# A fused Mamba, MLP and mixture layer on one core: weight splits moved in their block, narrow products with both weight halves side by side, last down products by tile

## The chip, the cores and the metric

The kernel runs on one NeuronCore of one Trainium2 chip. The metric is the device time of one execution in microseconds, as the median of several runs. Times inside an execution come from one profiled execution and are counted from the start of its span.

## The reference

The input is x, 8 sequences of 256 tokens with 512 channels, in float32.

```python
x = x + layernorm(attn(layernorm(x)))     # Mamba-2 block, then a gated MLP, each with a residual
x = x + layernorm(ffn(layernorm(x)))      # linear layer plus one of 4 rank-8 adapters for each token

# inside attn
zxbcdt = rmsnorm(h) @ w_in.T              # z, xs, B, C and dt (4 heads: 4 columns)
conv over 4 taps, silu; dt = softplus(dt + dt_bias)
chunks of 128 tokens: y = (C B' * decay) (x dt) + C state exp(cs) + D x
h = h + (y * silu(z)) @ w_out.T
h = h + (silu(h2 @ gate.T) * (h2 @ up.T)) @ down.T      # 1792 inner channels

# inside ffn
logits = x @ gate_w.T + bias; one_hot = argmax          # 4 columns
z = x @ lora_A.T                                        # 32 columns, masked by one_hot
out = x @ W_up.T + z_masked @ lora_B
```

The result must have about float32 precision. So every large product is made of float16 halves: each float32 operand is held as a high and a low float16 part, and a product is the sum of high x high, high x low and low x high.

## The kernel before

**Groups and steps.** A group is one sequence: 256 tokens, two tiles of 128. Three groups are in work at once, each in another branch. `steps` runs t from 1 to 9 with a = t (Mamba branch), b = t - 1 (MLP branch) and c = t - 2 (adapter branch); a branch whose group does not exist is left out. Step 1 has a = 1 and b = 0 and no c; step 8 has b = 7 and c = 6 and no a. Before step 1 the function `first` does the Mamba branch of group 0, and after step 8 the function `last` does what is left of groups 6 and 7.

**Blocks.** Each step has 14 blocks f, one for each 128 of the 1792 MLP channels. The order of work is written out by hand, once for each engine: a block has the MLP work of b first, then what the tables `A_AT`, `C_AT` and `NEXT_AT` name for this f. Nothing but this order and the semaphores schedules the work.

- TensorE, block f: `b_gu(b, f)`, 24 matmuls of 256 columns for gate and up (tiles gu0 and gu1, in turn); `b_down(b, f - 2)`, 6 matmuls of 512 columns, 3 for each token tile j, into acc0 and acc1; then the tables. After block 13 come the down products 12 and 13 together.
- ScalarE: `b_silu` (L782, sg from gu), `b_hi` (L792, high half of act), then the tables.
- VectorE: `b_prod` (L1220, sg times the up part), `b_lo` (L1225, low half of act), then the tables.

For one f this is a chain: TensorE's gate/up, silu on ScalarE, product on VectorE, high half on ScalarE, low half on VectorE, down product on TensorE. The gate/up product of block f waits for `b_prod` of block f - 2, since there are two gu banks.

**Weight splits.** The weights are scaled and split into halves on the chip: `upper_halves` (L630) on ScalarE and `lower_halves` (L1004) on VectorE, 56 units of 128x512. Part of them is made in `first`. The rest is made in step 1 by `prepare(f)`, called in each block f when a == 1: blocks 0 to 9 split gate and up of block f + 4 and down of block f + 1 (3 units), block 10 three down units, block 11 the four of the linear layer and the small gl_w, blocks 12 and 13 two units each of w_out (L643 and L1016), and block 13 the adapter matrices lora_b (`prep_lora`, VectorE, L990 to L996). A low half waits for its high half; in blocks 12 and 13 a high half also waits for the low half before it. Before the change `prepare(f)` stands between the MLP work of the block and the tables.

**The Mamba branch in a step.** TensorE makes the xs, B, C and z products (`a_in`, `a_z`, tile wa) in blocks 0 to 3, and in block 1 `a_dt`, the product for dt: for each token tile and each of the 4 k blocks three matmuls of 4 columns into tile wc. VectorE turns it into dts (`a_dtv`, L1096), ScalarE does abs, exp and ln (L707 to L709) in block 2, VectorE the rest of softplus (L1105 to L1116) and a_t. TensorE needs a_t for the two running sums in block 3 (`a_cs`, tri and a_t). These go over HBM and back, and ScalarE makes the decays in block 5 (L735, L725). VectorE multiplies them by dt (L1126) and by the attention products (`a_att`, L1135; the second in block 6). TensorE makes `a_state`, `a_y(0)` and `a_y(1)` in block 7; `a_y(1)` needs the second attention product. In block 7 VectorE forms y and, from group 2 on, its largest value, and from it y_diag (L1156, tile tok). TensorE spreads this over the partitions in block 8 (`a_y_spread`, ones x tok), so that y can be scaled and split in halves for the output projection (`a_o`, block 10). `a_hi1` and `a_lo1` (L662 and L1071, block 11) split the rows of the next group, which the DMA transposes into ht; TensorE needs ht in block 13 (`a_in(g + 1, 0)`). `a_hi2` and `a_lo2` (L767, L1208, block 12) do the same for h2t, which the next step's `b_gu` reads. `a_conv(g + 1, 0)` on ScalarE (L679, block 13) writes the buffer from which h2t was transposed, and waits for that transfer.

**The adapter branch.** `c_logits` (block 6) makes logits and z in one product with 36 columns, three matmuls for each tile and k. `c_route` (VectorE, block 6, L1308 to L1339) adds the bias, finds the first largest logit, masks z by `hot` and splits it into three bfloat16 parts, which TensorE transposes in block 7 (`c_zt`, L1720).

**The end.** In `last` VectorE waits for acc0 (semaphore `acc0_ready`), computes `b_mlp(7, 0)` (L1237), statistics and norms for tile 0 and then for tile 1, and the adapter branch of group 7 follows tile by tile.

The product functions before:

```python
PAIRS = [(0, 0), (0, 1), (1, 0)]
todo = [(lf[a], rt[b]) for lf, rt in zip(lefts, rights) for a, b in PAIRS]
for n, (lf, rt) in enumerate(todo):
    last = mm(dst, lf, rt, start and n == 0, stop and n == len(todo) - 1)
```

## Time and profile before

| | us |
|---|---|
| median of 3 runs (lowest, highest) | 768.98 (768.39, 773.36) |
| the profiled execution | 769.4 |
| its span | 767.7 |
| mean granted clock of TensorE in it | 0.986 of 2.4 GHz |
| TensorE busy | 733.9 |
| VectorE busy | 500.0 |
| ScalarE busy | 343.8 |

The span is the time between the first and last instruction; the profiled execution's own time is 1.7 us longer. A busy TensorE means that a matmul was in the array; a granted clock of 1.00 is 2.4 GHz and 0.50 is 1.2 GHz. All matmuls that go through the helper `mm` carry one line, L1478, so they are told apart by tile and shape. PE is TensorE, PEld its weight loads, DVE VectorE, ACT ScalarE, POOL GpSimd.

### The profile page before, as it was taken

To read this page: it belongs to the slowest core of one execution; us is meant where nothing else is said; L and a number is where in the kernel's file an instruction comes from. 1 tells how busy PE (TensorE), PEld (TensorE's weight loads), DVE (VectorE), ACT (ScalarE), POOL (GpSimd) and SP (SyncE) were. 2 spreads that over 40 slices of the span, in tenths; PEclk is the share of its full clock that TensorE was granted. 3 is DMA by queue.
4 is the path that set the end of the run, shared out by engine and by line. 5 is a ranking of instruction groups with operands and counts; after the bars stand their busy time and mean duration, and the time that the engine had idled before them with its cause. 6 is when DMAs were issued, how large, how long until landed. Compare 5 with 4: busy or idle time off the path is not lost.

```text
span 767.7 us, 14108 instructions
## 1 busy us (share of the span) xinstructions
PE 733.9 (96%) x5620; PEld 527.1 (69%) x5620; DVE 500.0 (65%) x1181; ACT 343.8 (45%) x671; POOL 133.1 (17%) x187
## 2 busy tenths in 40 slices
PE   4999898989999999999999999999999999999995
PEld 3867676667766877578666876578766876677752
DVE  5898868787655758367665757467674767365356
ACT  2854775446533373335633374245633265323211
POOL 2220211004110311105110311104210131001021
PEclk9999989999999999999999999999999999999997
DMA  8970010030204030040303120040303211032001
GB/s 310 386 255 1 2 55 1 1 83 29 56 1 83 28 83 3 0 111 3 81 1 56 56 58 27 1 110 2 83 1 41 71 35 22 1 83 49 9 1 55
DMA packets 61202, 44.82 MB, mean 58 GB/s; under 512 B 45848, under 2 KB 46032, under 8 KB 61136
## 3 DMA queue, kind: packets, MB, share of 16 engines
q1 hardware_dynamic: 61136, 43.92, 20.3%
q8 instruction: 44, 0.72, 0.4%
q14 instruction: 22, 0.18, 0.1%
HBM read 28.68 MB, written 4.22 MB: 43 GB/s over the span
## 4 chain that ended last, share of the span: by engine, by line
PE 70%; DVE 13%; ACT 8%; issue 4%; DMA 2%; SPq 1%; POOL 0%; ACTq 0%; DVEq 0%
PE gu L1478 30%; PE wa L1478 19%; PE acc L1478 15%; PE wc L1478 6%; ACT dec L735 2%; DVE xbc L1082 2%; DVE sg L1220 1%; DMA weights<-in_w_gate 1%; ACT L782 1%; DVE weights L1004 1%; DVE y L1143 1%; DMA ht<-ra 1%; ACT weights L630 1%; ACT sg L782 1%; DVE y_scales L1154 1%
## 5 line engine op out<-in xcount | busy, mean ns | idle before, releaser
L1478 PE MATMUL gu<-h2t,weights 128*128 128x256 f16 x2688 | 314.5, 274 | 1.0 <-DVE h2t L1214 1.0
L1478 PEld LDWEIGHTS gu<-h2t,weights 128*128 128x128 f16 x2688 | 263.4, 99 | 46.9 <-issue 5.1
L1478 PE MATMUL acc<-weights,act 128*128 128x512 f16 x672 | 161.7, 379 | 0.0
L1220 DVE SCALAR_TENSOR_TENSOR sg<-gu,bound,sg 128x256 f32<-128x256 f32 x112 | 53.3, 476 | 94.6 <-ACT sg L782 94.5
L782 ACT ACTIVATE sg<-gu,scale_inv 128x256 f32<-128x256 f32 x112 | 52.8, 471 | 134.5 <-PE gu L1478 134.3
L1478 PE MATMUL wa<-ht,weights 128*128 128x256 f16 x912 | 107.1, 275 | 4.0 <-DMA ht<-ra 3.7
L1478 PEld LDWEIGHTS acc<-weights,act 128*128 128x128 f16 x672 | 65.6, 98 | 57.7 <-DVE act L1225 0.3
L1478 PEld LDWEIGHTS wa<-ht,weights 128*128 128x128 f16 x912 | 89.7, 99 | 20.6 <-DMA ht<-ra 4.7
L792 ACT ACTIVATE act<-sg 128x256 f16<-128x256 f32 x112 | 46.6, 416 | 103.5 <-DVE sg L1220 103.5
L1225 DVE TENSOR_TENSOR act<-sg,act 128x256 f16<-128x256 f32 x112 | 49.7, 444 | 54.0 <-ACT act L792 54.0
L1082 DVE SCALAR_TENSOR_TENSOR xbc<-wa,conv_ws,xbc 128x253 f32<-128x253 f32 (+1 forms) x132 | 57.4, 476 | 1.6
L1004 DVE SCALAR_TENSOR_TENSOR weights<-weights,scale_v 128x512 f16<-128x512 f32 x56 | 39.9, 765 | 3.0 <-ACT weights L630 2.8
L491 POOL TENSOR_SCALAR small_c<-mv_c 128x2 f32<-128x2 f32 x21 | 4.0, 191 | 205.5 <-DVE mv_c L1026 205.5
L630 ACT ACTIVATE weights<-weights,scale_v 128x512 f16<-128x512 f32 x56 | 36.1, 708 | 0.7 <-DVE scale_v L953 0.7
L679 ACT ACTIVATE xbc<-wa,cols_t,conv_ws 128x256 f32<-128x256 f32 x48 | 24.3, 557 | 26.4 <-PE wa L1478 22.5
L520 POOL TENSOR_SCALAR y<-xbc,rows_t 128x256 f32<-128x256 f32 x28 | 30.7, 1109 | 26.0 <-ACT xbc L690 26.0
L1478 PE MATMUL wc<-weights,h3t 128*128 128x512 f16 x144 | 33.0, 379 | 0.0
L1478 PE MATMUL wa<-w_out_t,ra 128*128 128x512 f16 x144 | 32.1, 379 | 0.0
L491 POOL TENSOR_SCALAR small_a<-mv_a 128x2 f32<-128x2 f32 (+1 forms) x22 | 5.2, 235 | 150.9 <-DVE mv_a L1026 97.5
L760 ACT ACTIVATE hn<-h 128x512 f32<-128x512 f32 x16 | 10.1, 631 | 37.9 <-DVE h L1186 26.1
L512 POOL TENSOR_TENSOR hn<-tri,dts 128x512 f32<-128x512 f32 x16 | 17.9, 1140 | 48.2 <-DVE a_t L1116 48.2
L1478 PE MATMUL acc<-weights 128*128 128x128 bf16 x224 | 15.8, 228 | 10.4 <-DMA weights<-in_w_in 7.9
(242 smaller groups left out, 830.1 us busy)
## 6 DMA issues: line engine op xcount, KB each, us to landing
xa<-in_x SPq DMA_DIRECT2D x9, 512.0 KB, 3.7
ra<-cs_rows SPq DMA_DIRECT2D x7, 512.0 KB, 3.5
weights<-in_x SPq DMA_DIRECT2D x7, 512.0 KB, 3.8
out_x<-h SPq DMA_DIRECT2D x14, 256.0 KB, 2.1
weights<-in_w_in SPq DMA_DIRECT2D x5, 512.0 KB, 6.7
weights<-in_w_down SPq DMA_DIRECT2D x3, 768.0 KB, 12.9
weights<-in_w_gate SPq DMA_DIRECT2D x2, 1024.0 KB, 13.1
weights<-in_w_up SPq DMA_DIRECT2D x2, 1024.0 KB, 13.7
```

The lines of the kernel that those rows point to most:

```text
L512: nc.gpsimd.tensor_tensor(tdt[:, j], tri[:].unsqueeze(1).broadcast_to([P, H, P]), dts[:, 4, j].unsqueeze(2).broadcast_to([P, H, P]), ALU.m ...
L520: nc.gpsimd.tensor_scalar(y[:, h], xbc[:, 0], rowt[:, 4 + h:5 + h], None, ALU.mult)\
L630: nc.scalar.activation(Wh[:, u, 0], W[:, u + SHIFT], ACT.Copy, scale=sv[:, t:t + 1])\
L679: nc.scalar.activation(xbc[:, c], src[:, m * SEQ:(m + 1) * SEQ], ACT.Identity, bias=conv_b[:, c:c + 1], scale=cw[:, c * TAPS + TAPS - 1:c ...
L735: nc.scalar.activation(dec[:, j, h], ra[:, j, h], ACT.Relu, bias=cs_col[:, j, h:h + 1], scale=-1.0) .then_inc(sem("fall_ready"), 1)
L782: nc.scalar.activation(sg[:, f % 2], GU[f % 2][:, 0:SEQ], ACT.Silu, scale=inv_gate)\
L792: nc.scalar.activation(act[:, slot(f), 0], sg[:, f % 2], ACT.Copy)\
L1004: nc.vector.scalar_tensor_tensor(Wh[:, u, 1], W[:, u + SHIFT], sv[:, t:t + 1], Wh[:, u, 0], ALU.mult, ALU.subtract).then_inc(split, 1)
L1082: ins = nc.vector.scalar_tensor_tensor(xbc[:, c, late:], conv_in(g, c)[:, 0:SEQ - late], cw[:, c * TAPS + k:c * TAPS + k + 1], xbc[:, c, l ...
L1220: nc.vector.scalar_tensor_tensor(sg[:, f % 2], GU[f % 2][:, SEQ:2 * SEQ], up_to_act, sg[:, f % 2], ALU.mult, ALU.mult).then_inc(sem("prod_ ...
L1225: nc.vector.tensor_tensor(act[:, slot(f), 1], sg[:, f % 2], act[:, slot(f), 0], ALU.subtract)\
L1478: return nc.tensor.matmul(dst, left, right, start=start, stop=stop)
```

## The change

There are three edits.

1. `prepare(f)` on ScalarE and VectorE is called at the end of the block, behind the three tables, in step 1 (a == 1).
2. `a_dt` and `c_logits` use `narrow_product`. For each tile and k there are two matmuls in place of three: the high half of the tokens times both halves of the weights, which lie side by side (8 or 72 columns), and the low half of the tokens times the high half (4 or 36 columns) into the first part. The sum of the two parts is left to VectorE: a second operation in `a_dtv`, and in `c_route` a copy and an addition of 72 columns for each tile; the logits are then read from SBUF. The masking by `hot` is done in two operations, one for each tile.
3. For the last group the four down products left at the end are ordered by tile: (12, 0), (13, 0), (12, 1), (13, 1) in place of (12, 0), (12, 1), (13, 0), (13, 1).

```diff
@@ scalar and vector, step @@
-                    if a == 1:
-                        prepare(f)
                     if a is not None and f in A_AT:
                         A_AT[f](a)
                     if c is not None and f in C_AT:
                         C_AT[f](c)
                     if a is not None and a + 1 < GROUPS and f in NEXT_AT:
                         NEXT_AT[f](a + 1)
+                    if a == 1:
+                        prepare(f)
...
@@ vector, a_dtv @@
-                nc.vector.scalar_tensor_tensor(
-                    dts[:, 0], WC[:, 0:TILES * H].rearrange("p (t h) -> p t h", h=H), inv_dt,
-                    rowt[:, 8:12].unsqueeze(1).broadcast_to([P, TILES, H]), ALU.mult, ALU.add)\
+                src = WC[:, 0:2 * TILES * H].rearrange("p (t s h) -> p t s h", t=TILES, s=2)
+                chain_a(nc.vector.scalar_tensor_tensor(
+                    dts[:, 0], src[:, :, 1], inv_dt, rowt[:, 8:12].unsqueeze(1).broadcast_to([P, TILES, H]),
+                    ALU.mult, ALU.add))
+                nc.vector.scalar_tensor_tensor(dts[:, 0], src[:, :, 0], inv_dt, dts[:, 0], ALU.mult, ALU.add)\
                     .then_inc(sem("dtv_ready"), 1)
...
@@ vector, c_route @@
-                src = WC[:, 0:TILES * (E + E * R)].rearrange("p (t n) -> p t n", t=TILES)
+                n = E + E * R
+                src = WC[:, 0:2 * TILES * n].rearrange("p (t s n) -> p t s n", t=TILES, s=2)
+                chain_c(nc.vector.tensor_copy(z_low[:], src[:, :, 1]))
+                nc.vector.tensor_tensor(zs[:], src[:, :, 0], z_low[:], ALU.add).then_inc(sem("zs_ready"), 1)
+                dve.wait_ge(sem("zs_ready"), g + 1)
                 chain_c(nc.vector.scalar_tensor_tensor(
-                    lg[:], src[:, :, 0:E], inv_gl, rowt[:, 12:16].unsqueeze(1).broadcast_to([P, TILES, E]),
+                    lg[:], zs[:, :, 0:E], inv_gl, rowt[:, 12:16].unsqueeze(1).broadcast_to([P, TILES, E]),
                     ALU.mult, ALU.add))
-                nc.vector.tensor_copy(zs[:], src[:, :, E:]).then_inc(sem("zs_ready"), 1)
...
-                zv = zs[:].rearrange("p t (e r) -> p (t e) r", r=R)
-                hv = hot[:].rearrange("p t e -> p (t e)").unsqueeze(2).broadcast_to([P, TILES * E, R])
-                chain_c(nc.vector.tensor_tensor(zv, zv, hv, ALU.mult))
+                for t in range(TILES):
+                    zv = zs[:, t, E:].rearrange("p (e r) -> p e r", r=R)
+                    ins = nc.vector.tensor_tensor(zv, zv, hot[:, t].unsqueeze(2).broadcast_to([P, E, R]), ALU.mult)
+                    chain_c(ins, wait=t == TILES - 1)
...
@@ tensor @@
+            def narrow_product(dst, n, lefts, rights):
+
+                for k, (lf, rt) in enumerate(zip(lefts, rights)):
+                    mm(dst, lf[0], rt, k == 0, False)
+                    last = mm(dst[:, 0:n], lf[1], rt[:, 0], False, k == len(lefts) - 1)
+                return last
...
-            def b_down(g, f):
+            def b_down(g, f, js=range(TILES)):
...
-                for j in range(TILES):
+                for j in js:
...
-                last.then_inc(sem("down_done"), 1)
+                    if j == TILES - 1:
+                        last.then_inc(sem("down_done"), 1)
...
-                if b is not None:
+                if b is not None and alone(b):
+
+                    for f, j in ((FBLK - 2, 0), (FBLK - 1, 0), (FBLK - 2, 1), (FBLK - 1, 1)):
+                        b_down(b, f, [j])
+                elif b is not None:
                     for f in range(FBLK - BEHIND, FBLK):
                         b_down(b, f)
```

**Order on VectorE, step 1, block 2.** Before: the splits of weights, then the convolution of xbc, then softplus on dts and a_t.

```order
L1004 SCALAR_TENSOR_TENSOR weights<-weights,scale_v 128x512 x3
L1082 SCALAR_TENSOR_TENSOR xbc<-wa,conv_ws,xbc 128x253 x2
L1082 SCALAR_TENSOR_TENSOR xbc<-wa,conv_ws,xbc 128x254 x2
L1082 SCALAR_TENSOR_TENSOR xbc<-wa,conv_ws,xbc 128x255 x2
L1105 TENSOR_SCALAR dts<-dts 128x8
L1110 TENSOR_TENSOR dts<-dts 128x8
L1108 SCALAR_TENSOR_TENSOR dts<-dts 128x8 x3
L1111 TENSOR_TENSOR dts<-dts 128x8
L1112 SCALAR_TENSOR_TENSOR dts<-dts 128x8
L1113 TENSOR_TENSOR dts<-dts 128x8
L1115 SCALAR_TENSOR_TENSOR dts<-dts 128x8
L1116 TENSOR_TENSOR a_t<-dts,neg_a 128x8
```

Now the same stretch of VectorE (the lines have moved by 1 to 3):

```order
L1083 SCALAR_TENSOR_TENSOR xbc<-wa,conv_ws,xbc 128x253 x2
L1083 SCALAR_TENSOR_TENSOR xbc<-wa,conv_ws,xbc 128x254 x2
L1083 SCALAR_TENSOR_TENSOR xbc<-wa,conv_ws,xbc 128x255 x2
L1108 TENSOR_SCALAR dts<-dts 128x8
L1113 TENSOR_TENSOR dts<-dts 128x8
L1111 SCALAR_TENSOR_TENSOR dts<-dts 128x8 x3
L1114 TENSOR_TENSOR dts<-dts 128x8
L1115 SCALAR_TENSOR_TENSOR dts<-dts 128x8
L1116 TENSOR_TENSOR dts<-dts 128x8
L1118 SCALAR_TENSOR_TENSOR dts<-dts 128x8
L1119 TENSOR_TENSOR a_t<-dts,neg_a 128x8
L1005 SCALAR_TENSOR_TENSOR weights<-weights,scale_v 128x512 x3
```

The three splits have moved from ahead of the convolution to behind a_t. The same holds for every block of step 1.

**Order on ScalarE, step 1, from block 12 on.** Before (w_out_t are the high halves of w_out, xbc<-hn the rows for h2t, xbc<-wa the first taps of group 2):

```order
L643 ACTIVATE w_out_t<-w_out_t,scale_v 128x512 x2
L767 ACTIVATE xbc<-hn,sumsq 128x512 x2
L782 ACTIVATE sg<-gu,scale_inv 128x256
L792 ACTIVATE act<-sg 128x256
L643 ACTIVATE w_out_t<-w_out_t,scale_v 128x512 x2
L679 ACTIVATE xbc<-wa,cols_t,conv_ws 128x256 x2
```

Now:

```order
L768 ACTIVATE xbc<-hn,sumsq 128x512 x2
L644 ACTIVATE w_out_t<-w_out_t,scale_v 128x512 x2
L783 ACTIVATE sg<-gu,scale_inv 128x256
L793 ACTIVATE act<-sg 128x256
L680 ACTIVATE xbc<-wa,cols_t,conv_ws 128x256 x2
L644 ACTIVATE w_out_t<-w_out_t,scale_v 128x512 x2
```

In block 12 the rows for h2t come first, and in block 13 the taps, which wait for h2t's transfer, now stand ahead of the last two halves of w_out.

**Order on TensorE, the last down products of group 7**, with the semaphores that they wait for. Before:

```order
L1478 MATMUL acc<-weights,act 128x512 [waits act_ready]
L1478 MATMUL acc<-weights,act 128x512 x5
L1478 MATMUL acc<-weights,act 128x512 [waits act_ready]
L1478 MATMUL acc<-weights,act 128x512 x5
L1478 MATMUL wa<-weights,h3t 128x512 [waits zt_ready]
```

Now:

```order
L1484 MATMUL acc<-weights,act 128x512 [waits act_ready]
L1484 MATMUL acc<-weights,act 128x512 x2
L1484 MATMUL acc<-weights,act 128x512 [waits act_ready]
L1484 MATMUL acc<-weights,act 128x512 x2
L1484 MATMUL acc<-weights,act 128x512 [waits act_ready]
L1484 MATMUL acc<-weights,act 128x512 x2
L1484 MATMUL acc<-weights,act 128x512 [waits act_ready]
L1484 MATMUL acc<-weights,act 128x512 x2
L1484 MATMUL wa<-weights,h3t 128x512 [waits zt_ready]
```

Two runs of six have become four of three: the first two end tile 0, the others tile 1.

## Rows read from the trace of the kernel before

**Rows 1.** The page: busy time of each engine, share of the span, instructions.

```profile
PE 733.9 (96%) x5620; PEld 527.1 (69%) x5620; DVE 500.0 (65%) x1181; ACT 343.8 (45%) x671; POOL 133.1 (17%) x187
```

**Rows 2.** Waits of TensorE's matmuls: us in total, times, longest.

```profile
PE wa L1478 <- DMA ht<-ra: 3.7, 2, 3.1
PE wc L1478 <- DVE a_t L1116: 3.3, 1, 3.3
...
PE wa L1478 <- DVE dec L1135: 2.2, 1, 2.2
```

**Rows 3.** Waits of TensorE's weight loads, same columns.

```profile
PEld wa L1478 <- DVE tok L1156: 3.5, 6, 0.6
```

**Rows 4.** Waits of VectorE between 73 and 167 us, same columns.

```profile
DVE sg L1220 <- ACT sg L782: 6.8, 6, 2.5
DVE act L1225 <- ACT act L792: 6.8, 14, 0.5
DVE dec L1126 <- ACT dec L725: 2.5, 1, 2.5
```

**Rows 5.** TensorE in time: start, length (us), instruction, idle before.

```profile
94.74 0.60 PE L1478 MATMUL wc<-tri,a_t 128*8 128x128 f32 x2 [3.30 <-DVE a_t L1116]
...
95.71 5.11 PE L1478 MATMUL gu<-h2t,weights 128*128 128x256 f16 x24
...
119.83 1.13 PE L1478 MATMUL wa<-dec,tok 128*128 128x512 f32 x2 [2.21 <-DVE dec L1135]
...
186.42 0.39 PE L1478 MATMUL wc<-tri,a_t 128*8 128x128 f32 x2
```

**Rows 6.** VectorE in time, steps 1 and 2.

```profile
92.71 0.17 DVE L1105 TENSOR_SCALAR dts<-dts 128x8 f32<-128x8 f32 x1 [0.78 <-ACT dts L709]
...
117.10 2.08 DVE L1004 SCALAR_TENSOR_TENSOR weights<-weights,scale_v 128x512 f16<-128x512 f32 x3 [0.19 <-ACT weights L630]
...
166.86 0.48 DVE L1220 SCALAR_TENSOR_TENSOR sg<-gu,bound,sg 128x256 f32<-128x256 f32 x1
...
185.67 0.17 DVE L1116 TENSOR_TENSOR a_t<-dts,neg_a 128x8 f32<-128x8 f32 x1
```

**Rows 7.** ScalarE in time, step 1.

```profile
86.51 1.93 ACT L630 ACTIVATE weights<-weights,scale_v 128x512 f16<-128x512 f32 x3
...
162.12 1.02 ACT L679 ACTIVATE xbc<-wa,cols_t,conv_ws 128x256 f32<-128x256 f32 x2 [0.98 <-DMA h2t<-xbc]
```

**Rows 8.** Windows of 1 us: busy TensorE, granted clock, DMA share, GB/s.

```profile
122.00:123.00 1.00, 1.00 (x7) 0.50 0.00 0
...
154.00:155.00 1.00, 0.00 (x0) 1.00 1.05 191
```

**Rows 9.** TensorE in time, step 3.

```profile
260.07 0.74 PE L1478 MATMUL wc<-dt_w,ht 128*128 128x4 f16 x24
260.68 2.78 PE L1478 MATMUL gu<-h2t,weights 128*128 128x256 f16 x24
...
288.18 0.76 PE L1478 MATMUL wc<-gl_w,h3t 128*128 128x36 f16 x24
...
300.67 0.49 PE L1478 MATMUL wa<-tok,ones 128*128 128x128 f32 x2
```

**Rows 10.** VectorE in time, step 3, route and the next product.

```profile
291.94 0.22 DVE L1308 SCALAR_TENSOR_TENSOR logits<-wc,scale_inv,rows_t 128x8 f32<-128x8 f32 x1
...
292.34 0.15 DVE L1312 TENSOR_REDUCE mx<-logits 128x2 f32<-128x8 f32 x1
...
293.79 0.23 DVE L1330 TENSOR_TENSOR zs<-zs,hot 128x64 f32<-128x64 f32 x1
...
295.00 0.48 DVE L1220 SCALAR_TENSOR_TENSOR sg<-gu,bound,sg 128x256 f32<-128x256 f32 x1
```

**Rows 11.** The chain that ended last: start, us, what.

```profile
736.80 3.25 PE acc L1478 x15
```

**Rows 12.** VectorE in time, the end.

```profile
740.17 0.75 DVE L1237 SCALAR_TENSOR_TENSOR weights<-acc,bound,h1b 128x512 f32<-128x512 f32 x1 [1.44 <-PE acc L1478]
```

More of the change, by code:

```diff
@@ L209, in build @@
         lg = sb("logits", [P, TILES, E])
-        zs = sb("zs", [P, TILES, E * R])
-        zr = sb("zr", [P, TILES, E * R])
+        zs = sb("zs", [P, TILES, E + E * R])
+        z_low = sb("z_low", [P, TILES, E + E * R])
+        zr = z_low[:, :, E:]
         zp = sb("z_parts", [P, TILES, 8, E * R], BF16)
@@ L1335, in c_route @@
                 prev(g, 1, 1, dve, sem("zt_ps_ready"))
[L1336 to L1339 removed]
+                chain_c(nc.vector.tensor_copy(zp[:, :, 2:5], copies(zs[:, :, E:], 3)))
+                chain_c(nc.vector.tensor_tensor(zr, zs[:, :, E:], zp[:, :, 2], ALU.subtract))
+                chain_c(nc.vector.tensor_copy(zp[:, :, 0:2], copies(zr, 2)))
+                nc.vector.tensor_tensor(zp[:, :, 5], zr, zp[:, :, 0], ALU.subtract)\
                     .then_inc(sem("zm_ready"), 1)
@@ L1380, in step @@
                         NEXT_AT[f](a + 1)
+                    if a == 1:
+                        prepare(f)
                 if a is not None:
@@ L1560, in a_dt @@
                 for j in range(TILES):
-                    last = split_product(WC[:, j * H:(j + 1) * H], [tokens(ht, k, j) for k in range(KB)],
-                                         [[dt_w[:, s, k] for s in range(2)] for k in range(KB)])
+                    last = narrow_product(WC[:, 2 * j * H:2 * (j + 1) * H], H, [tokens(ht, k, j) for k in range(KB)],
+                                          [dt_w[:, :, k] for k in range(KB)])
                 last.then_inc(sem("dt_ps_ready"), 1)
@@ L1709, in c_logits @@
                         pe.wait_ge(sem("last_t3_split"), j + 1)
-                    last = split_product(WC[:, j * n:(j + 1) * n], [tokens(h3t, k, j) for k in range(KB)],
-                                         [[gl_w[:, s, k] for s in range(2)] for k in range(KB)])
+                    last = narrow_product(WC[:, 2 * j * n:2 * (j + 1) * n], n, [tokens(h3t, k, j) for k in range(KB)],
+                                          [gl_w[:, :, k] for k in range(KB)])
                 last.then_inc(sem("lg_ps_ready"), 1)
```

11 lines of the change are left out of this document (2 added, 9 removed).

## The prediction

> **What bounds the kernel now.** I read the page first: TensorE is busy 96% of the span [rows 1], so a microsecond counts only where TensorE waits, works at half its clock, or does less. Then the waits of TensorE: apart from loads at the start and the tail there are three long ones, on a_t, on dec and on the transposed ht [rows 2]; all three lie in step 1, the step in which the weights are still being split. The waits of the weight loads show one more, small and regular: 3.5 us in 6 pieces on tok, written at L1156 [rows 3]. That is y_spread (L1478, ones x y_diag), once in each of steps 2 to 7. So in these steps VectorE's chain up to y_diag ends just after TensorE gets there. Everywhere else in steps 2 to 8 TensorE sets the pace.
>
> The times below are of the profiled execution: 767.7 us of span, 769.4 us in all, 0.4 above the median of 768.98. I work out differences and take them off the median.
>
> **The weight splits at the end of each block (step 1).** Nothing is added: each block of 3 splits (2.08 us on VectorE [rows 6], 1.93 us on ScalarE [rows 7]) is done later within its block. TensorE needs a gate or up slot four blocks and a down slot three blocks after its split, so a move within the block does not make it wait. What moves up is the other branch's work.
>
> First wait, 3.30 us on a_t [rows 2, 5]. The chain to a_t in block 2 passes one block of splits on each engine. ScalarE's softplus steps start 1.84 us earlier, and VectorE's first step after them (92.71, after 0.78 us of waiting for ScalarE [rows 6]) comes at about 90.95. TensorE starts at 93.0 instead of 94.74. That is 1.76 us, and with 0.2 us less of its own work before, its wait is still 1.8 us.
>
> Second wait, 2.21 us on dec [rows 5]. The second attention product on VectorE stands behind the splits of block 6, which start at 117.10 and take 2 us [rows 6]. Before it, ScalarE's exponentials in block 5 no longer stand behind splits, and going block by block ScalarE and VectorE gain 1.9 us up to there. The product ends about 115.6 and y(1) starts near 115.7, 4.1 us earlier. But TensorE, pulled forward too and at full clock, would be there at 113.1: its wait is 2.6 us, not gone.
>
> Third wait, 3.1 us on ht [rows 2]. The low halves of the next group's rows stand behind four splits in block 11, and after the move behind none. In my walk VectorE is 3 to 5 us ahead by then, ht lands about 148.1, and TensorE waits 0.3 us for it, so it starts step 2 earlier by much more than VectorE does: its first gate/up product could start 6.5 us earlier.
>
> What is late next: VectorE. Its work in step 1 is the same, it can only give up idle time: 6.8 us before sg and 2.5 us before dec, while the 6.8 us in 14 pieces before act are a round trip to ScalarE that stays [rows 4]. Two things take some of it back. In block 10 the splits used to fill the wait for the output projection, and now follow it. In block 13 ScalarE now does the next group's first taps before the last w_out halves; these taps wait for the landing of h2t (0.98 us even before [rows 7]), and VectorE's low halves and all of the lora preparation queue behind them. From both I get VectorE's first product of step 2 (166.86 [rows 6]) 2.9 us earlier, not 6.5. VectorE then works nearly without a break to a_t of step 2 (185.67 [rows 6]), which TensorE meets at 186.42 [rows 5] with some 0.5 us to spare. With the extra operation of a_dtv (0.25 us) a_t comes 2.65 us earlier; TensorE, 6.7 us earlier, waits 3.4 us and goes on at 183.2. The term is **-3.2 us**. Ends: 0, if each gain only turns into a wait, and -6.7, if TensorE keeps all of it.
>
> The clock. Behind the first wait 24 gate/up matmuls took 5.11 us instead of 2.78 [rows 5, 9], and behind the second the granted clock read 0.50 (1.2 GHz); behind the third, the second longest, it stayed at 1.00 (2.4 GHz) [rows 8]. So a wait of this length may or may not cost clock. (The Trainium skill, "TensorE: Matmul & The Clock Gate", section "What's actually happening", says that the same kernel slows differently from run to run, by the phase at its start; the trace agrees in that like waits had unlike outcomes.) My walk has three candidates: 2.6 us before y(1), about 2.4 us before the last down product of step 1 (the low half in block 13), and 3.4 us on a_t of step 2. A spell at half clock costs between nothing, where a wait follows, and the 2.3 us by which the gate/up block grew. I take **+1.7 us** for one that counts; ends 0 and +5.
>
> **Products with both halves side by side.** For dt, 24 matmuls of 4 columns take 0.61 us from their start to that of the next block [rows 9], 25 ns each. Now 16 of 4 or 8 columns: 8 x 25 = 0.20 us less. The logits' 24 matmuls of 36 columns take 0.76 us with the end of the last [rows 9], about the same spacing. Of the new 16, 8 have 72 columns; 256 columns take 109 ns (24 in 2.78 us with the end of the last [rows 9], 2.62 without), so 72 take between 25 and 109 ns, by proportion 31. That saves 0.15 us; at 109 ns it would cost 0.47.
>
> (The Trainium skill, same page, section "Back-to-back issue gap", says that in a stream of weight loads and matmuls the loads count too, about 81 ns a pair at 128 columns. By that the 128 pairs saved would be worth 10.4 us; the trace has whole pairs at 25 ns.)
>
> The price is on VectorE. a_dtv has a second operation, about 0.25 us, hidden before z(0) in steps 3 to 7 (ScalarE waits for TensorE there). In c_route the logits and the copy take 0.40 us before (291.94 to 292.34 [rows 10]). Now there are a copy of 72 columns and an addition, each like an operation on these tiles with its wait, 0.26 us, and the logits from SBUF, 0.20: 0.72 in all, +0.32. The masking by hot, 0.26 us in one operation before, is two of half the width, the first without a wait: +0.07. Together **+0.39 us** per step; ends 0.1 (the operations overlap) and 0.8 (each new one costs a full 0.26). VectorE's next product follows without a gap (295.00 [rows 10]), then y, y_top and y_diag, for which TensorE already waits [rows 3], and which it starts at 300.67 [rows 9]. So in steps 2 to 7 all of it lands on the path: 6 x 0.39 = **+2.3 us**, and the 0.15 us of the logits only lengthens TensorE's wait there, 0.58 to about 1.1 us by the weight loads. Saved on the path: dt in steps 3 to 7, 5 x 0.20 = **-1.0 us**; the logits of step 8, which has no y_spread, and of the tail, **-0.25 us**. At the start the dt product's gain and the second a_dtv operation cancel.
>
> **Last down products tile by tile.** acc0 was ready after 15 matmuls, which take 3.25 us, 0.217 each [rows 11], and VectorE, idle 1.44 us, waited for it at 740.17 [rows 12]. Now it is ready after 12: 0.65 us earlier, if the last block's act is there: VectorE ended its low half 1.44 us before 740.17, at 738.73 [rows 12], and TensorE comes to it 9 matmuls after 736.80, at 738.75. VectorE then works without a gap for several microseconds, and the later waits of TensorE shorten with it: **-0.65 us**. Ends: 0 and -0.7. In the tail c_route's extra 0.39 us is hidden behind 18 matmuls of the linear product.
>
> **Sum.** -3.2 + 1.7 + 2.3 - 1.0 - 0.25 - 0.65 = -1.1 us: 768.3 for the profiled execution, 767.9 for the median.
>
> **The rivals.** (a) VectorE keeps up: its waits in step 1 vanish, a_t of step 2 is not late, TensorE keeps 6.7 us and no clock is lost. For it: 9.3 us of idle time that can go [rows 4]. Against it: VectorE's unbroken work from the low halves to a_t, and the taps waiting for h2t. -6.7 + 2.3 - 1.25 - 0.65 = -6.3: 762.7 us. (b) Slower: the waits collect in one place, a_t of step 2, where TensorE stands 3.4 us and the clock falls behind it as it did at 94.74, after another fall at y(1). It decides once the clock costs 2.8 us more than nothing; with 5 us it gives +2.2, 771.2 us. For it: two of the three waits of step 1 cost clock. Against it: a fall inside step 1 is partly taken up by the next wait. (c) c_route's operations overlap, or y_spread has slack that the trace hides: without the +2.3, 765.6 us. Against it: six like waits. (d) Whole pairs cost what the page says: up to 10.4 us less, 759 us; the rows speak against it.
>
> **How the numbers follow.** Forecast 0.60, (a) 0.11, (b) 0.16, (c) 0.11, (d) 0.02. The forecast's own range is 766.2 (no clock lost) to 770. To hold 8 in 10 with parts of (a), (b) and (c) on both sides I take 764.5 to 771. One per cent, 7.7 us, is about what a measurement of this kernel can tell from no change. Below 761.3 us only (d) and a generous (a) lead: 0.04. Above 776.7 would take a wait that I have not found: 0.03. Within 1%: 0.93.
>
> **What would show it.** In the changed profile: the wait on a_t in step 1 near 1.8 us and a new one on a_t near 3.4 us in step 2; the wait before y(1) still there; ht no longer waited for; the weight loads' waits on tok, six pieces, near 1.1 us each; the time from one y_spread to the next in steps 3 to 7 longer by 0.2 us; the last group's first DVE result 0.65 us closer to the last gate/up block. I am wrong if step 2 starts a_t without a wait (then (a)), if the tok waits stay at 0.6 us (then (c)), or if the clock stays below 1.00 for over 6 us behind new waits (then (b)).

## The result, and the profile after

The changed kernel took 774.39 us in the median of 8 runs (772.72 to 775.99), beside 771.75 us for the kernel before (8 runs, 768.39 to 773.36): ratio 1.0042, 95% interval 1.0025 to 1.0060. That is slower by 1.9 to 4.6 us; the prediction had 1.1 us faster. The three runs of before shown ahead of the prediction lay 2.8 us below that median. All comparisons below are ratios to runs of before on the same chip at the same time; 0.001 is 0.77 us.

The page of the kernel after, its first lines, beside [rows 1]: VectorE is busy 5.7 us longer and GpSimd 3.4 us, though GpSimd's program is the same.

```profile
span 774.0 us, 13868 instructions
...
PE 735.8 (95%) x5492; PEld 525.9 (68%) x5492; DVE 505.7 (65%) x1205; ACT 343.2 (44%) x671; POOL 136.5 (18%) x187
```

The waits of TensorE after (matmuls, then weight loads; total, times, longest), beside [rows 2, 3]. The wait on ht in step 1 is all but gone (0.2 us); a_t in step 1 is shorter, dec (before y(1)) longer; act, a second a_t and the matmuls' waits on tok are new.

```profile
PE wa L1484 <- DVE tok L1159: 4.3, 6, 0.7
...
PE wc L1484 <- DVE a_t L1119: 3.4, 2, 2.2
...
PE wa L1484 <- DVE dec L1138: 2.7, 1, 2.7
PE acc L1484 <- DVE act L1228: 2.2, 1, 2.2
...
PEld wa L1484 <- DVE tok L1159: 7.3, 6, 1.2
```

TensorE in time after, steps 1 and 2, beside [rows 5].

```profile
72.72 5.41 PE L1484 MATMUL gu<-h2t,weights 128*128 128x256 f16 x48 [0.98 <-DVE h2t L1217]
96.44 0.39 PE L1484 MATMUL wc<-tri,a_t 128*8 128x128 f32 x2 [2.21 <-DVE a_t L1119]
121.27 2.08 PE L1484 MATMUL wa<-dec,tok 128*128 128x512 f32 x2 [2.74 <-DVE dec L1138]
155.42 2.79 PE L1484 MATMUL wa<-ht,weights 128*128 128x256 f16 x24 [0.21 <-DMA ht<-ra]
161.67 2.39 PE L1484 MATMUL acc<-weights,act 128*128 128x512 f16 x6 [2.16 <-DVE act L1228]
189.96 0.39 PE L1484 MATMUL wc<-tri,a_t 128*8 128x128 f32 x2 [1.20 <-DVE a_t L1119]
```

Step 1 starts at 72.72; before it started at 69.73, with this row:

```profile
69.73 3.45 PE L1478 MATMUL gu<-h2t,weights 128*128 128x256 f16 x30 [0.98 <-DVE h2t L1214]
```

Over the profiled runs of this study, whose code up to there differs at most in dt, this start lies anywhere from 69.73 to 74.17. So times in step 1 are counted from it. From it to the product on a_t of step 2 it is 117.24 us, before 186.42 - 69.73 = 116.69: the wait on ht went and nothing was gained. From one y_spread to the next, called a period below, it is 87.70 us (305.00 to 392.70) against 87.42 before; two of the five periods after were longer, 88.76 and 88.12, each with a wait on ht (0.90 and 0.24 us), and one of before, 88.20. And the granted clock, beside [rows 8], is down in a third place, behind the new wait on act (windows of 1 us, same columns):

```profile
122.00:123.00 1.00, 1.00 (x2) 0.50 0.06 16
154.00:155.00 1.00, 1.00 (x6) 1.00 0.87 162
163.00:164.00 1.00, 1.00 (x4) 0.50 0.59 227
```

By windows of 2 us the clock was low for 3.4 us in each of the three places, before for 6.8 behind a_t and 3.4 behind dec: 10.2 us either way.

VectorE in time after, step 3, beside [rows 10]: from the end of the attention product to its next gate product 3.54 us (295.78 to 299.32), before 3.06 (291.94 to 295.00).

```profile
295.78 0.23 DVE L1312 COPY z_low<-wc 128x72 f32<-128x72 f32 x1
296.04 0.23 DVE L1313 TENSOR_TENSOR zs<-wc,z_low 128x72 f32<-128x72 f32 x1
296.31 0.23 DVE L1315 SCALAR_TENSOR_TENSOR logits<-zs,scale_inv,rows_t 128x8 f32<-128x8 f32 x1
296.57 0.16 DVE L1318 TENSOR_REDUCE mx<-logits 128x2 f32<-128x8 f32 x1
...
298.04 0.29 DVE L1335 TENSOR_TENSOR zs<-zs,hot 128x32 f32<-128x32 f32 x2
...
299.32 0.48 DVE L1223 SCALAR_TENSOR_TENSOR sg<-gu,bound,sg 128x256 f32<-128x256 f32 x1
```

VectorE's waits after between 73 and 167 us, beside [rows 4]. Of the 6.8 us on sg 0.2 are left, but now VectorE waits longer for ScalarE's splits and for the output projection. All its waits in that stretch, the smaller ones too, add up to 22.5 us before and 22.0 after.

```profile
DVE act L1228 <- ACT act L793: 6.8, 14, 0.5
DVE w_out_t L1017 <- ACT w_out_t L644: 3.6, 3, 2.1
DVE weights L1005 <- ACT weights L631: 3.5, 3, 1.5
DVE dec L1129 <- ACT dec L726: 2.9, 1, 2.9
DVE h L1191 <- PE wa L1484: 2.7, 1, 2.7
```

And its splits took longer. VectorE's splits of gate, up, down and the linear layer as a group (busy us, mean ns of one), of the kernel before, then of the kernel after:

```profile
L1004 DVE SCALAR_TENSOR_TENSOR weights<-weights,scale_v 128x512 f16<-128x512 f32 x56 | 39.9, 765 | 3.0 <-ACT weights L630 2.8
```

```profile
L1005 DVE SCALAR_TENSOR_TENSOR weights<-weights,scale_v 128x512 f16<-128x512 f32 x56 | 42.3, 806 | 4.5 <-ACT weights L631 4.4
```

The chain at the end, beside [rows 12], first the last gate/up block of before, then the rows after: VectorE starts on acc0 5.74 us after the start of the last gate/up block (740.13), before 6.16 (740.17 - 734.01). But the clock in the tail then was down for 6.8 us, before for 3.4, and the whole tail came out no shorter.

```profile
734.01 2.78 PE L1478 MATMUL gu<-h2t,weights 128*128 128x256 f16 x24
```

```profile
740.13 2.78 PE L1484 MATMUL gu<-h2t,weights 128*128 128x256 f16 x24
...
745.87 0.75 DVE L1240 SCALAR_TENSOR_TENSOR weights<-acc,bound,h1b 128x512 f32<-128x512 f32 x1 [1.01 <-PE acc L1484]
```

### The profile page after: what moved, and what is told of

Same layout as the page of the kernel before. It is cut to its first block, busy times and chain, and to the rows that moved or that the text cites. A ratio compares the mean times of both kernels' runs of the same rounds, so it can differ in the third digit from the quotient of the medians.

```text
span 774.0 us, 13868 instructions
## 1 busy us (share of the span) xinstructions
PE 735.8 (95%) x5492; PEld 525.9 (68%) x5492; DVE 505.7 (65%) x1205; ACT 343.2 (44%) x671; POOL 136.5 (18%) x187
## 4 chain that ended last, share of the span: by engine, by line
PE 63%; DVE 19%; ACT 8%; issue 5%; DMA 2%; SPq 1%; POOL 0%; ACTq 0%; DVEq 0%
PE gu L1484 26%; PE wa L1484 17%; PE acc L1484 14%; PE wc L1484 6%; DVE weights L1005 3%; DVE xbc L1083 3%; ACT dec L736 2%; DVE sg L1223 2%; DVE y L1146 1%; ACT act L793 1%; DMA ht<-ra 1%; DMA weights<-in_w_in 1%; ACT L783 1%; DVE y_scales L1157 1%; ACT sg L783 1%
## 5 line engine op out<-in xcount | busy, mean ns | idle before, releaser
L1005 DVE SCALAR_TENSOR_TENSOR weights<-weights,scale_v 128x512 f16<-128x512 f32 x56 | 42.3, 806 | 4.5 <-ACT weights L631 4.4
L1484 PE MATMUL acc<-weights 128*128 128x128 bf16 x224 | 16.9, 237 | 10.5 <-DMA weights<-in_w_in 9.1
```

The costliest lines, as they stand in the source:

```text
L1005: nc.vector.scalar_tensor_tensor(Wh[:, u, 1], W[:, u + SHIFT], sv[:, t:t + 1], Wh[:, u, 0], ALU.mult, ALU.subtract).then_inc(split, 1)
L1484: return nc.tensor.matmul(dst, left, right, start=start, stop=stop)
```

## The experiments

### The parts one by one

**The move of the splits alone**: in both step() functions

```
-                    if a == 1:
-                        prepare(f)
                     if a is not None and f in A_AT:
...
                         NEXT_AT[f](a + 1)
+                    if a == 1:
+                        prepare(f)
```

> Only the first part of the change: each block's weight splits of step 1 at the end of the block, on ScalarE and VectorE; products and tail as before. Theory M (the gains inside step 1 cancel, because VectorE loses what it was to gain): 0 to +1 us beside before, one value +0.5. In the trace: waits on a_t in step 1 near 2.2 us, before y(1) near 2.7, ht 0.2 instead of 3.1, a new one near 2.2 on act before the last down product of step 1 and one near 1 on a_t of step 2; from the first gate/up product of step 1 to the cumulative product of a_t in step 2 117.2 us, against 116.7 before. From one y_spread to the next 87.4 as before, tok waits 0.58. Rival F (the recorded forecast): -1.5 us (-3.2 for the move, +1.7 of clock), the 116.7 us shrink to about 115. Rival S (the late start of step 1 in the trace of after, 72.72 against 69.73, comes from the change): nothing of this part runs before that point, so 0 from it here.

Measured: ratio 1.0009 (0.9992 to 1.0026). Waits: a_t 1.47, before y(1) 2.74, ht 0.20, act 2.17, a_t of step 2 0.93; from the start of step 1 to the product on a_t of step 2 116.67 us (before 116.69), periods 87.42. Theory M holds, with 0.5 us less on that stretch than the 117.2 it had and a shorter wait on a_t; the recorded -1.5 us (0.9981) lies outside the interval. The row on which the account of the forecast rests is VectorE's first product of step 2, here 97.72 us after the start of step 1 (71.16); before it was 97.13 (166.86 - 69.73 [rows 6]):

```profile
168.88 0.47 DVE L1220 SCALAR_TENSOR_TENSOR sg<-gu,bound,sg 128x256 f32<-128x256 f32 x1
...
187.83 0.39 PE L1478 MATMUL wc<-tri,a_t 128*8 128x128 f32 x2 [0.93 <-DVE a_t L1116]
```

Between these two ends VectorE was busy 73.6 us before and 74.5 here, and its waits add up to 22.5 and 22.1 us.

**The last down products tile by tile alone** (b_down takes js; the last step calls it as in the change):

> Only the last group's last down products tile by tile. Theory M: VectorE's first result 5.74 us behind the start of the last gate/up block instead of 6.16, so -0.4 us, of which the clock in the tail may take back all: -0.4 to +0.2 us over the whole. Rival F (forecast): -0.65 us. Rival K (the order of the four pieces itself costs clock each time): the half clock spell of the tail is near 7 us long instead of 3.4, and the end comes 31.4 us behind the last gate/up block instead of 31.2. Nothing before the last block changes.

Measured: 0.9984 (0.9966 to 1.0001). The first result came 5.74 us behind the last gate/up block, as expected, and here the clock did not fall before the last product: from that block to the last matmul group 23.41 us, before 25.51. K is out. M's 0.4 and the forecast's 0.65 both fit the interval; the profile of this one run gained more because of the clock.

**The dt product alone**: narrow_product, and a_dtv in two operations.

> Only the dt product with both halves side by side, and the second operation of a_dtv. Theory M and forecast F agree: 0.41 us instead of 0.61 from its start to the next block, in the free steps 3 to 7, so -1.0 us in all, and the y_spread period falls from 87.42 to 87.2; the tok waits stay at 0.58. Rival N (narrow matmuls with unequal widths save nothing where the wait for y_spread follows VectorE): the period stays 87.42 and the time is the same, 0. Rival S (the dt edit delays the start of step 1): +2 to +3 us, the first gate/up product of step 1 at about 72.7 instead of 69.7.

Measured: 0.9996 (0.9978 to 1.0013); three of five periods 87.22 or 87.23 (the others 87.34 and 87.51), so 0.20 us each, as both theories had it; N is out. The start of step 1 was 72.63 without any cost in the median: S is out.

**The logits alone**: narrow_product in c_logits, the c_route of the change.

> Only the logits with both halves side by side, and the longer c_route on VectorE. Theory M: c_route 0.47 us longer, all of it on the path in the six steps with a y_spread: the period 87.42 + 0.47 = 87.9, tok waits of the weight loads 1.2 us, 6 x 0.47 - 0.3 (step 8 and tail) = +2.5 us. Forecast F: 6 x 0.39 - 0.25 = +2.1. Rival C (c_route's operations are hidden): 0 or -0.3 us, tok waits at 0.58.

Measured: 1.0054 (1.0035 to 1.0074); periods 87.90, tok waits 7.2 us in 6. C is out. The trace has 6 x 0.48 = 2.9 us, the ratio 4.2 (2.7 to 5.7). So two more runs: the same kernel again, and

```
-                src = WC[:, 0:2 * TILES * n].rearrange("p (t s n) -> p t s n", t=TILES, s=2)
-                chain_c(nc.vector.tensor_copy(z_low[:], src[:, :, 1]))
-                nc.vector.tensor_tensor(zs[:], src[:, :, 0], z_low[:], ALU.add)
+                src = WC[:, 0:TILES * n].rearrange("p (t n) -> p t n", t=TILES)
+                chain_c(nc.vector.tensor_copy(z_low[:], src))
+                nc.vector.tensor_tensor(zs[:], src, z_low[:], ALU.max)
```

with TensorE's 24 products as before.

> The logits edit once more, the same kernel as the first time. Theory M (6 x 0.48 on the path, the rest was scatter): +2.9 us, ratio near 1.0038, its interval overlapping the first one (1.0035 to 1.0074). Rival N (something more, such as half clock spells that the shape of the products brings): +4 us again, ratio 1.005 or more.

> Only VectorE's longer c_route (a copy of 72 columns, a second operation on it, the logits from SBUF, the masking in two), with TensorE's 24 products of the logits as before; the second operation is a maximum of the product with its own copy, so the values are the same. Theory M (all the cost of the logits edit is VectorE's operations): y_spread period 87.9, tok waits 1.1 to 1.2 us, 6 x 0.48 = 2.9 us and 0.3 for step 8 and the tail: +2.9 to +3.3, no better than the logits edit. Rival N (the narrow products cost 1 us or more themselves): +1.5 to +2.9 here, and at least 1 us less than the logits edit beside it. Rival X (the trace hides slack): 0 to +1 us.

Measured: the repeat 1.0034 (1.0014 to 1.0053), VectorE's operations alone 1.0039 (1.0022 to 1.0056), periods 87.90 in both. All three intervals hold 2.9 us (ratio 1.0038), so the excess of the first need be no more than scatter; X is out. N, 1.005 or more for the repeat, is not excluded by that interval, but the run without the narrow products cost as much as the repeat with them. The logits' narrow products save nothing in a step that has a y_spread: weight loads wait on tok (total, times, longest) with VectorE's operations alone, then with the narrow products too:

```profile
PEld wa L1482 <- DVE tok L1157: 6.4, 6, 1.1
```

```profile
PEld wa L1482 <- DVE tok L1157: 7.2, 6, 1.2
```

The parts sum to 0.0009 - 0.0016 - 0.0004 + 0.0044 (mean of two) = 0.0033; the whole is 0.0042. They add up within their intervals.

### c_route moved out of the way

```
-            C_AT = {6: lambda g: c_logits(g), 7: lambda g: c_zt(g),          (TensorE)
+            C_AT = {6: lambda g: c_logits(g), 8: lambda g: c_zt(g),
-                    6: lambda g: c_route(g), 12: ...                          (VectorE)
+                    7: lambda g: c_route(g), 12: ...
```

and c_zt of ScalarE from 7 to 8; the second kernel has the logits edit besides.

> The kernel before with c_route on VectorE moved from block 6 to block 7, behind a_y_top, and c_zt on TensorE and ScalarE from block 7 to block 8; no operation is changed. Theory M (VectorE's chain c_route, y, y_top, y_diag is what TensorE waits for at y_spread): the waits on tok vanish, the y_spread period falls by the 0.58 us of a wait from 87.42 to 86.85, 6 x 0.58 = -3.5 us, 767.5 beside 771. Rival W (another wait takes its place: c_route's result is late for c_zt in block 8, or the y halves late for the output projection in block 10): the period stays within 0.1 of 87.42 and a new wait of 0.5 us or more stands on zm or y_halves; 0 to +2 us.

> The same move of c_route and c_zt, with the logits of both halves side by side and the longer c_route. Theory M: its 0.47 us more on VectorE are now hidden, and the 0.15 to 0.3 us that the narrow products save show: the y_spread period 86.6 to 86.85, ratio to before as of the move alone or up to 1.5 us better (766 to 767.5), where the same edit without the move cost 3.9 us. Rival V (VectorE as a whole is the bound in these steps, so its extra 0.47 us cost the same wherever they stand): 2 to 3 us slower than the move alone, period 0.48 longer than there. Rival N (the 72 column products themselves cost time on TensorE): the same 2 to 3 us slower, but with TensorE's block of logits longer than 0.76 us and no wait.

Measured: 1.0323 (1.0298 to 1.0348) and 1.0367 (1.0342 to 1.0392), period 91.8 and 92.15. M is out in both runs. The move of c_route itself, TensorE's waits, and one of them in time:

```profile
PE wc L1720 <- DVE z_parts L1339: 15.4, 6, 2.6
```

```profile
311.25 0.40 PE L1720 MATMUL wc<-ident,z_parts 128*128 128x128 bf16 x4 [2.58 <-DVE z_parts L1339]
311.49 4.44 PE L1478 MATMUL gu<-h2t,weights 128*128 128x256 f16 x24
```

TensorE now stands 2.6 us before c_zt, and the gate/up block behind that takes 4.44 us in place of 2.78; together that is the 4.4 us of the longer period. W named the place but not the size: it had 0 to +2 us, and 25 were measured. The tok waits stay, 3.4 us in 6: in block 7 VectorE now waits for ScalarE's sigmoid, which ScalarE does behind its copy of the state, which waits for TensorE:

```profile
302.51 0.48 DVE L1220 SCALAR_TENSOR_TENSOR sg<-gu,bound,sg 128x256 f32<-128x256 f32 x1 [2.73 <-ACT sg L782]
```

So before the change c_route bound y_spread with little to spare. Counted from the gate/up block of block 7 (288.79 before, 296.54 here), y_spread comes 11.88 us later before, 11.65 here: with all 3.06 us of c_route out of its way it gained 0.23 us, while 0.48 us more cost 0.48. And the longer c_route costs again here, before c_zt (0.33 us a period, 3.4 us by the two ratios): Rival V in kind, though it had 0.48 a period; N, which wanted no wait, is out.

### Which blocks' splits

The blocks whose splits go to the end, the rest in front, as in

```
+                    if a == 1 and f in (6, 11):
+                        prepare(f)
```

> The weight splits at the end of the block only in blocks 6 and 11 of step 1; in the others in front, as in the kernel before. Theory M: block 11 alone takes away the wait of 3.1 us on ht, block 6 part of the 2.2 us before y(1); VectorE's waits for ScalarE's splits in blocks 3, 4 and 10 do not arise and the block behind a_t takes 2.7 us as before. TensorE then waits 1 to 2 us on a_t of step 2, so -1 to -2.5 us: from the first gate/up product of step 1 to the cumulative product of a_t in step 2 114.5 to 115.7 us instead of 116.7. Rival Z (the end of step 1 is bound by VectorE's work alone, whatever its order): 116.7 and 0 us.

> The splits at the end of the block in block 6 only. Theory Y (the wait of 2.2 us before y(1), and the half clock spell behind it, are what can be had): the wait goes, no spell at 120 to 125; TensorE and VectorE both stand 2 us earlier from there, the wait of 3.1 us on ht stays or grows; -1.5 to -3.5 us beside before. Rival B (block 6 alone moves TensorE only, and the wait on ht in step 1 grows by as much): ht waits 5 us, 0 to -1 us.

> The splits at the end of the block in block 11 only. Theory M: the wait of 3.1 us on ht vanishes (0.2 to 0.5 left), VectorE's first product of step 2 comes about 2.5 us earlier, TensorE waits 0 to 1 us on a_t of step 2; from the first gate/up product of step 1 to the cumulative product of a_t in step 2 113.5 to 114.5 us instead of 116.7 (less where the clock does not fall), -2 to -3 us in the median. Rival B (the gain of blocks 6 and 11 together came from block 6): the wait on ht goes but a wait on a_t of step 2 of 2 us or more takes its place, 0 to -1 us.

> The splits at the end of the block in blocks 6 to 13, in front in 0 to 5. Theory E (what spoils the whole move is the early blocks: a_t earlier puts splits of 3.6 and 3.1 us beside GpSimd in front of the second attention product, whose wait stays 2.7 us): the wait before y(1) goes here, -2 to -4 us beside before as with blocks 6 and 11. Rival L (the late blocks 10, 12 and 13 spoil it, where VectorE waits 1.4 and 2.1 us for ScalarE's splits): a wait on a_t of step 2 of 2 to 3 us, 0 to -1 us.

> The splits at the end of the block in all blocks except 2 and 5, the two in which they would run beside GpSimd. Theory G (what this slowing and the waits for ScalarE's splits behind a_t cost is what kept the whole move from gaining): the splits of blocks 2 and 5 take 2.08 us, those of block 3, now first beside GpSimd's mask product, 2.1 to 2.7; -1.5 to -3 us beside before, so 2 us or more better than the whole move, which measured +0.7. Rival Q (the loss is in blocks 10 and 13, where the splits wait for ScalarE and for the first taps): 0 to +1 us as with the whole move.

> The splits at the end of the block in blocks 0 to 11, those of w_out and the lora preparation in blocks 12 and 13 in front as before. Theory M: the wait of 2.1 us that VectorE has on ScalarE's w_out halves behind the first taps in block 13 goes; -1 to -2 us beside before. Rival R (the new wait of 2.2 us of TensorE on the last act of step 1 takes it back): within 0.5 us of the whole move, 0 to +1 us beside before.

Waits of TensorE in us, D the time from the start of step 1 to the product on a_t of step 2 in the one profiled run, "low" the number of spells at half clock within it, each 3.4 or 6.8 us long (waits of about 1 us on h2t are left out, and in "all" and "0 to 11" two of 0.7 and 0.8 us on GpSimd's hn and ScalarE's tok):

| at the end | ratio (95%) | a_t | y(1) | ht | act | a_t, step 2 | D | low |
|---|---|---|---|---|---|---|---|---|
| none (before) | 1 | 3.3 | 2.2 | 3.1 | - | - | 116.7 | 2 |
| all | 1.0009 (0.9992-1.0026) | 1.5 | 2.7 | 0.2 | 2.2 | 0.9 | 116.7 | 2 |
| 0 to 11 | 0.9983 (0.9963-1.0003) | 1.5 | 2.7 | 0.3 | 2.1 | - | 118.0 | 2 |
| all but 2, 5 | 0.9995 (0.9976-1.0014) | 3.3 | - | 0.2 | 2.2 | 2.6 | 113.9 | 1 |
| 6 to 13 | 0.9982 (0.9966-0.9999) | 3.3 | - | 0.2 | 2.2 | 0.9 | 113.6 | 2 |
| 6, 11 | 0.9958 (0.9938-0.9978) | 3.3 | - | - | 2.2 | - | 110.6 | 0 |
| 6 | 0.9966 (0.9951-0.9982) | 3.3 | - | 3.9 | - | - | 114.1 | 2 |
| 11 | 0.9986 (0.9969-1.0004) | 3.3 | 2.2 | - | 1.6 | - | 115.2 | 2 |

Block 6 carries the gain (theory Y: the wait goes; the wait on ht stayed, 3.9 us, which B had too, but the ratio is Y's); block 11 alone shows none that can be told (-1.1, within -2.4 and +0.3): Rival B's outcome, though the wait on a_t of step 2 which B wanted did not come; its place was taken by 1.6 us on act. For "6, 11" Rival Z's 116.7 us are out and the gain is 3.2 us (1.7 to 4.8), at least the 1 to 2.5 of theory M, whose wait on a_t of step 2 did not come. For blocks 6 to 13 neither theory fits whole: the wait before y(1) went as E has it, but of its 2 us at least only 1.4 (0.1 to 2.6) came, and L's wait on a_t of step 2 is 0.9 us. For "all but 2, 5" theory G's gain of 1.5 us or more is not shown (-0.4, within -1.9 and +1.1, so Rival Q's 0 fits as well), though the splits of blocks 2 and 5 did take 2.08 us per block. "0 to 11" can't be told from either of its theories. D follows the clock as much as the waits: its 110.6 was the fastest of 12 runs and had no spell at all, so 6.1 us there stand beside 3.2 in the ratio.

Why the whole move keeps the wait before y(1) can be read in VectorE's order: between the two attention products there is always one block of splits. Before it was block 6's, in front of the second product; at the end of the blocks it is block 5's, behind the first. Only with block 6 at the end and block 5 in front is there none, and in those four rows the wait is gone. The row "all but 2, 5" then ends as the recorded rival (b) had it: the waits collect at a_t of step 2, 2.6 us, with the clock at 0.50 behind it, and no gain is left that the median shows. Between "6, 11", "6 to 13" and "0 to 11" the intervals touch; how much each late block takes back stays open.

### Splits beside GpSimd

> The splits at the end of each block, and in step 1 (the group with index 1) GpSimd's a_tdt and a_xw write 1 column of 128 in each row, so the rest of dt times mask and of w times tokens is left out there. Theory G (VectorE's splits are slowed while GpSimd works): the splits behind a_t of step 1 take 2.08 us instead of 3.63 and those of the block of y(1) near 2.1 to 2.5 instead of 3.14 (a_ce is left in); from the first gate/up product of step 1 to the cumulative product of a_t in step 2 115 to 116 us instead of 116.7. Rival P (they are slow for another reason, such as the PSUM or a DMA): 3.6 and 3.1 us as before.

The rows that raised it: VectorE's splits (here 3 in a row) of block 2, and GpSimd's mask product. In the kernel before they meet in part:

```profile
96.17 2.69 DVE L1004 SCALAR_TENSOR_TENSOR weights<-weights,scale_v 128x512 f16<-128x512 f32 x3
...
94.77 2.22 POOL L512 TENSOR_TENSOR hn<-tri,dts 128x512 f32<-128x512 f32 x2 [7.38 <-DVE a_t L1116]
```

in the kernel after in full, and both are longer:

```profile
96.31 3.63 DVE L1005 SCALAR_TENSOR_TENSOR weights<-weights,scale_v 128x512 f16<-128x512 f32 x3
...
96.47 2.92 POOL L513 TENSOR_TENSOR hn<-tri,dts 128x512 f32<-128x512 f32 x2 [7.26 <-DVE a_t L1119]
```

and with GpSimd's product cut to one column:

```profile
95.75 2.07 DVE L1006 SCALAR_TENSOR_TENSOR weights<-weights,scale_v 128x512 f16<-128x512 f32 x3
...
95.91 1.30 POOL L513 TENSOR_TENSOR hn<-tri,dts 128x4 f32<-128x4 f32 x2 [6.36 <-DVE a_t L1118]
```

2.07 us again, and the splits of block 5 take 2.52 instead of 3.14: theory G holds for the splits, P is out. D fell to 112.9 us (one spell at half clock instead of two), 3.8 less than with the whole move. Up to VectorE's first product of step 2 its work fell from 74.5 to 72.2 us and its waits from 22.1 to 20.8, 1.3 of that before the output projection. This is one run (768.84 us) of a kernel that leaves out GpSimd's work too, so what the collision costs the whole is not measured by it.

That product then came 93.96 us after the start of step 1 (72.71), 3.2 earlier than before; and in the run "all but 2, 5", which leaves GpSimd's work as it is but keeps the splits of these two blocks away from it, 94.90 (start 70.26), 2.2 earlier. The rows, of the run with GpSimd's product cut and of "all but 2, 5":

```profile
166.67 0.47 DVE L1222 SCALAR_TENSOR_TENSOR sg<-gu,bound,sg 128x256 f32<-128x256 f32 x1
```

```profile
165.16 0.48 DVE L1222 SCALAR_TENSOR_TENSOR sg<-gu,bound,sg 128x256 f32<-128x256 f32 x1
```

### The gains together

```
+                    if a == 1 and f in (6, 11):        (both engines; in front for the others)
+                        prepare(f)
...
+                for f, j in ((FBLK - 2, 0), (FBLK - 1, 0), (FBLK - 2, 1), (FBLK - 1, 1)):
+                    b_down(b, f, [j])
```

with the dt product of the change, and the logits and c_route of the kernel before.

> Three edits together on the kernel before: the splits at the end of the block in blocks 6 and 11 only, the dt product with both halves side by side, the last down products tile by tile; the logits and c_route as before. Theory M (the gains add up: 3.8 for the splits of 6 and 11, about 1 for dt, 0.4 to 2 for the tail): 5 to 6.5 us below before, 765 to 766.5 us, ratio 0.992 to 0.994; y_spread period 87.2, tok waits 0.6. Rival A (the gains overlap in the clock: parts of them are the same luck with half clock spells): -3 to -4 us, 768.

Measured: 765.55 us, ratio 0.992 (0.9898 to 0.9943), 6.2 us below before and so about 9 below the change. Periods 87.22. M holds; A, 0.995 to 0.996, is outside the interval (the wait on a_t in step 1 is still there, 3.8 us, and so is one of 2.2 on act).

## Why the prediction was wrong, step by step

- **Direction and size.** Forecast -1.1 us, measured +3.2 (1.9 to 4.6). Two of its terms failed; of the others the traces show the size of dt and two thirds of the last down products, and no ratio can tell them from nothing. That the time stays within 1% was right.
- **The splits, -3.2 for the move and +1.7 of clock.** This is the step that failed most: -1.5 forecast, +0.7 measured (-0.6 to +2.0). The waits of TensorE were named rightly: 1.8 forecast on a_t and 1.5 to 2.2 found, 2.6 before y(1) and 2.7, 0.3 on ht and 0.2, 2.4 before the last down product and 2.2. What failed is "VectorE's first product of step 2 2.9 us earlier". It came at 168.88 with the move alone, 97.72 us after the start of step 1, where it was 97.13 before: 0.6 us later. I treated VectorE's work as constant and 2.9 us of its idle time as what could be given up.
- **Why that step failed.** Neither held: VectorE's busy time up to there went from 73.6 to 74.5 us, and its waits only changed their names, 22.5 us to 22.1 (sg 6.8 to 0.2, but ScalarE's splits 3.9 to 7.2 and the output projection 1.3 to 2.7). Of the 3.5 us between forecast and outcome 0.9 are thus work and 2.5 waits.
- **The splits beside GpSimd.** Behind the work stand two blocks of splits that now fall beside GpSimd, 3.63 us for 2.69 and 3.14 for 2.08, most of the growth of the 56 splits from 39.9 to 42.3 us. In the two runs above in which they meet it less or not at all the product came 2.2 ("all but 2, 5") and 3.2 us earlier than before, near the forecast, but by another way: the work was down to 72.2 us in both, and the waits were still 21.7 and 20.8, not 2.9 less than 22.5. So the idle time was not given up there either, and the collision comes on top of that; what it costs in the median stays open, as the ratio of "all but 2, 5" shows no gain. Where only block 6, or 6 and 11, moved, the waits did fall, to 18.5 and 16.5 us. The wait on a_t of step 2, 3.4 us forecast and 0.9 found, is no better for that: TensorE came late too. The first sign of the collision stood in the trace of before, in the 2.69 us of one block where the other blocks of three took 2.08.
- The Trainium skill, "SBUF — State Buffer", section "SBUF: two separate sides", has the rule that I did not weigh: a VectorE operation with two SBUF inputs and a GpSimd operation that reads SBUF lock each other out of a shared port for whole instructions. The runs agree in kind. Run one after the other, three splits (2.08) and two mask products (2.22) would take 4.3 us; overlapped both were done 3.63 us after VectorE's start, so part of GpSimd's time ran beside VectorE.
- **c_route, +2.3.** The mechanism was right, all of it lands on the path through y_spread in six steps. The term was too small: 0.48 us per step measured against 0.39; of it the front part is 0.39 against my 0.32 (the logits from SBUF cost 0.26 us, like the copy and the addition of 72 columns, not the 0.20 at which I put them). Six of them are 2.9 us. Rival (c) is out.
- **dt, -1.0.** Periods 0.20 shorter, as forecast; -0.3 (-1.7 to +1.0) in the ratio. Rival (d) is out: whole pairs cost what the rows said.
- **Logits of step 8 and the tail, -0.25.** Too small to be seen.
- **Last down products, -0.65.** The first result came 0.42 us earlier: TensorE came to the last block's products of the first tile before that block's act was there (the forecast had it there with 0.02 us to spare), and the 18 products took 4.28 us instead of 4.05. Alone the edit gave -1.2 (-2.6 to +0.1).
- **The clock.** Charged at +1.7; in the two profiles step 1 lost nothing (10.2 us low in both), the tail 3.4 us more at half clock. Between runs of near kernels the spells in step 1 number 0 to 3, so nothing shows this term as a cost of the change rather than scatter. The walk behind the -3.2 has one more weak point: its five waits of TensorE, 1.8, 2.6, 0.3, 2.4 and 3.4, add up to 10.5 us, where before had 8.6, so its gain had to come from TensorE running at full clock. With the move alone the waits were 9.0, and TensorE was busy 107.7 us up to a_t of step 2, before 108.1, and 104.0 in "6, 11", which had no spell: of those 4.1 us 0.4 came back. Rival (b) had the direction and not the cause: in the profile after, a_t of step 2 was waited for 1.2 us and the clock behind it stayed at 1.00. (a) is out.
- **The range.** 764.5 to 771 was taken around the median of three runs that lay 2.8 us low; the scatter of the start of step 1 alone is over 4 us. Even the right difference, +3.2, on that median gives 772.2, 2.2 below what was measured; the range should have held the scatter of a median of three.

## What to carry to other kernels

Moving work within an engine keeps its amount only if what runs beside it stays the same: look at what GpSimd is doing at the new place, and in the trace for one row of a group that is longer than its fellows. Where several waits can be removed by the same move, remove them one at a time: block 6 alone was worth more than all fourteen together. On an engine whose chain is met just in time, added operations cost their full time in every step (0.48 us here), although taking away 3.06 us of the same chain gained 0.23.

## What the hardware did that was not expected

- VectorE's three splits take 2.08 us alone and 3.63 beside GpSimd's mask product, which itself goes from 2.22 to 2.92 us.
- VectorE's copy of 72 columns from PSUM, the addition behind it and the logits' operation on 8 columns of SBUF cost 0.26 to 0.27 us each from start to start, though they differ in width (295.78, 296.04, 296.31, 296.57); the operations of 8 and 2 columns that follow cost 0.20 each.
- Like kernels start step 1 between 69.73 and 74.17 us, and like waits of 2.2 to 3.3 us go with the full clock or with 3 to 7 us at 0.50 (0.50 is 1.2 GHz, 1.00 is 2.4 GHz): behind the 3.3 us on a_t the clock stayed at 1.00 in the run of "6, 11" and fell in that of before.
